# Second attention of a vision tower: where VectorE gives slots to routed tokens, and where TensorE turns the third group's outputs back

## The chip, the cores and the metric

The kernel runs on one core of a Trainium2 chip. Its time is the device time of one execution in microseconds (us), and a smaller time is better. Five engines work side by side and wait for one another through semaphores: TensorE (PE in the profile, with its weight loads as PEld), VectorE (DVE), ScalarE (ACT), GpSimd (POOL) and the queue of SyncE (SP), which issues DMAs.

## The reference, cut to what matters

32 sequences of 256 tokens with 256 features pass a token mixer, a first attention with 16 heads, and then a block with a latent attention and a mixture of eight experts. A class token is put ahead of each sequence, so a sequence has 257 rows. The change lies in the latent attention (called the second attention here), whose stage also does the routing for the experts.

```python
def _mla(h, Wq, Wdkv, Wuk, Wuv, Wo):
    q = (h @ Wq).reshape(B, S, HEADS, hd)          # 16 heads of 16
    c = h @ Wdkv                                   # latent of 128
    k = (c @ Wuk).reshape(B, S, HEADS, hd)
    v = (c @ Wuv).reshape(B, S, HEADS, hd)
    scores = jnp.einsum('bqhd,bkhd->bhqk', q, k) / jnp.sqrt(...)
    scores = jnp.where(causal, scores, -1000000000.0)
    a = jax.nn.softmax(scores, axis=-1)
    out = jnp.einsum('bhqk,bkhd->bqhd', a, v).reshape(B, S, D)
    return out @ Wo

def _moe(h, gate_w, w1, w2):
    logits = t @ gate_w
    top_v, top_i = jax.lax.top_k(logits, TOP_K)    # 2 of 8 experts
    gates = jax.nn.softmax(top_v, axis=-1)
    ...                                            # silu(t w1) w2, combined by the gates
x = x + _mla(_rmsnorm(x, g1), Wq, Wdkv, Wuk, Wuv, Wo)
x = x + _moe(_rmsnorm(x, g2), gate_w, w1, w2)
```

## The kernel before, in words

The program has stages that follow one another: constants and the token mixer with the first attention (to about 1700 us of the trace), a short stage for the class tokens, the second attention (`latent_attention`, about 1780 to 2890 us), the loading of the experts' weights, the experts, and the final output.

`latent_attention` goes through 32 samples (sequences). Samples 0 to 2 and 29 to 31 are written out; samples 3 to 28 run in a loop with two samples in its body. Each engine has its own `sample` function, and the order of the calls in it is the order of that engine's instructions; nothing else sets it. What keeps the engines in step are waits on semaphores.

The 16 heads of a sample are four groups (0 to 3) of four heads. A group goes through this chain:

- TensorE `scores` (L2118 mask, L2124 products) puts the scores of a group into PSUM banks 0 to 3. It first waits until ScalarE has read the previous group out of these banks (`exp_done`), the first two banks and the last two separately.
- VectorE `maxima` (L1852, two reductions) takes the row maxima out of the banks.
- TensorE `turn_maxima` (L2133) transposes them; VectorE `lower_queries` (L1857) adds them to the queries.
- TensorE `mask_keys` (L2139) and `lowered_scores` (L2148, L2153) compute the transposed scores less their maxima.
- ScalarE `powers` (L1722, L1723) takes the exponentials in two halves. `scores` of the next group can fill the banks from then on.
- TensorE `weigh` (L2168, L2171) applies them to the values, ScalarE `copy_output` (L1712) copies the result, TensorE `turn_back` (L2190) transposes it back, VectorE `divide` (L1863, L1865) divides by the row sums.

Between the links of this chain stand parts of other samples: TensorE computes the next sample's latents, keys, values and queries (`turn` L2022, `latent` L2029, `keys` L2040, `values`, `queries`), and for the sample before its output projection (`turn_output` L2197, `output` L2205) and its routing (`turn_tokens` L2079, `logits`, `counts`). `turn_back` and `divide` of groups 2 and 3 of a sample are done during group 0 of the next one.

The routing of the sample before the current one is a side line: VectorE `norm_tokens` (L1887) writes the normalised tokens, GpSimd `token_copy` (L1624, L1626) doubles them, VectorE `give_slots` (L1936 to L1947) turns ranks and counts into row numbers and gate weights, and GpSimd `scatter` (L1640) writes the rows to memory with four indirect DMAs, each issued when the one before has landed. GpSimd then goes on in its queue: `roots` (L66) and `keep` (L1613, L1614), which copy a sample's normalised rows away. VectorE's `normalise` (L1819, L1824) of the sample two ahead waits for both. VectorE's `choose` (L1899 to L1924), which ranks the experts, stands in group 2; `result` (L1875, L1876) stands ahead of it.

Of the kernel before, what the change touches and what calls it, by code (L numbers as in the profile page):

```python
# [1458 lines left out]
def latent_attention(nc, v, a, nb):  # L1459
# [5 lines left out]
    with ExitStack() as ctx:  # L1465
# [74 lines left out]
        def need(eng, sem, n):  # L1540

            if not isinstance(n, int) or n > 0:
                eng.wait_ge(sem, n)
# [12 lines left out]
        def sent(n):  # L1556

            return 64 * n + 32
# [237 lines left out]
        def _(dve):  # L1796
# [48 lines left out]
            def maxima(i, g, first=None):  # L1845

                dve.wait_ge(s_done, 4 * i + g + 1)
                for t in range(LT):
                    if t and first:
                        first(i)  # L1850
                    cols = slice(0, SEQ) if t else slice(SEQ, SEQ + 1 + P)
                    dve.tensor_reduce(nm[:, t, :, DK], ps[:, 0:4, cols], AX.X, ALU.max,  # L1852
                                      negate=True).then_inc(max_done, 1)

            def lower_queries(i, d, g):
                dve.wait_ge(nm_done, 4 * i + g + 1)
                dve.tensor_tensor(qx[:, g % 2], ps[:, OB + g % 2, L:2 * L], qT[:, d, g], ALU.add).then_inc(qx_done, 1)  # L1857

            def divide(i, g):
                bank = (BB, BA, BB, BB)[g]  # L1860
                dve.wait_ge(back_done, 4 * i + g + 1)
                out = ps[:, bank, 0:L].rearrange("p (t h r) -> p t h r", t=LT, h=4)
                dve.reciprocal(rec[:, g % 2], out[:, :, :, DK]).then_inc(rec_done, 1)  # L1863
                dve.wait_ge(rec_done, 4 * i + g + 1)
                dve.tensor_tensor(on[:, :, 4 * DK * g:4 * DK * (g + 1)].rearrange("p t (h d) -> p t h d", h=4),  # L1865
                                  out[:, :, :, 0:DK], rec[:, g % 2].unsqueeze(3).to_broadcast([P, LT, 4, DK]),
                                  ALU.mult).then_inc(on_done, 1)
# [14 lines left out]
            def norm_tokens(i, e, rows):  # L1882
                dve.wait_ge(r_rooted, i)
                if not isinstance(i, int) or i >= 3:
                    dve.wait_ge(rows_out, sent(i - 3))
                for t in range(LT):
                    dve.scalar_tensor_tensor(tn[:, e, 0, t, 0:MODEL], rows[:, t], ms[:, 2, t:t + 1], v.g2[:], ALU.mult,  # L1887
                                             ALU.mult).then_inc(z_done, 1)
# [37 lines left out]
            def place(i, d):  # L1926
                dve.wait_ge(counted, i - 1)
                need(dve, placed, i - 2)
                cnt = ps[:, CNB, FREE:FREE + (LT + 1) * NEXP].rearrange("p (t e) -> p t e", e=NEXP)
                dve.tensor_tensor(pos[:], cnt[:, 0:LT], v.fill[:, d].unsqueeze(1).to_broadcast([P, LT, NEXP]),  # L1930
                                  ALU.add).then_inc(slot_step, 1)
                dve.tensor_tensor(v.fill[:, 1 - d], cnt[:, LT], v.fill[:, d], ALU.add).then_inc(placed, 1)
# [16 lines left out]
            def sample(i, d, before, behind):  # L1949
                j, e = i + 1, 1 - d  # L1950
                maxima(i, 0, (lambda i: place(i, d)) if before >= 2 else None)
                lower_queries(i, d, 0)
                if before:
                    divide(i - 1, 2)
                    divide(i - 1, 3)
                if behind:
                    class_keys(j, e)
                if before:
                    norm_tokens(i, e, v.xcls if before == 1 else x)
                if before >= 2:  # L1960
                    give_slots(i, d)
                maxima(i, 1)
                lower_queries(i, d, 1)
                if behind:
                    last_value(j, e)
                if behind == 2:
                    norm_stats(i + 2, d)
                if before:
                    result(i - 1, e)
                maxima(i, 2, read_logits if before else None)  # L1970
                lower_queries(i, d, 2)
                if before:
                    choose(i)
                divide(i, 0)
                maxima(i, 3)
                lower_queries(i, d, 3)
                divide(i, 1)
                if behind:
                    last_key(j, e)
                if behind == 2:  # L1980
                    normalise(i + 2, d)
                if before:
                    mean_square(i)
# [32 lines left out]
        def _(pe):  # L2016
            def turn(j):
                pe.wait_ge(hn_done, LT * j + LT)
                need(pe, on_done, 4 * j - 6)
                for k in range(KT):  # L2020
                    for t in range(LT):
                        last = pe.transpose(ps[:, BA, k * L + t * P:k * L + (t + 1) * P], hn[:, t, k * P:(k + 1) * P],  # L2022
                                            v.ident[:])
                last.then_inc(hn_T, 1)
# [103 lines left out]
            def turn_maxima(i, g):  # L2128
                n = 4 * i + g
                pe.wait_ge(max_done, LT * n + LT)  # L2130
                need(pe, o_copied, n - 1)
                for t in range(LT):
                    last = pe.transpose(ps[:, OB + g % 2, L + t * P:L + (t + 1) * P],  # L2133
                                        nm[:, t].rearrange("p h r -> p (h r)"), v.ident[:])
                last.then_inc(nm_done, 1)
# [38 lines left out]
            def turn_back(i, g, more):  # L2174
                pe.wait_ge(o_copied, 4 * i + g + 1)
                bank = (BB, BA, BB, BB)[g]
                if g == 0:
                    need(pe, base_done, i)
                elif g == 1 and more:
                    pe.wait_ge(q_copied, 2 * i + 3)  # L2180
                elif g == 1:
                    pe.wait_ge(zT_done, i)
                elif g == 2 and more:
                    pe.wait_ge(q_copied, 2 * i + 4)
                elif g == 2:
                    pe.wait_ge(on_done, 4 * i + 1)
                elif g == 3:
                    pe.wait_ge(on_done, 4 * i + 3)
                for t in range(LT):
                    last = pe.transpose(ps[:, bank, t * P:(t + 1) * P], oa[:, g % 2, t * P:(t + 1) * P], v.ident[:])  # L2190
                last.then_inc(back_done, 1)
# [17 lines left out]
            def sample(i, d, before, behind):  # L2209
                j = i + 1  # L2210
                scores(i, d, 0, counts if before >= 2 else None)
                if before:
                    weigh(i - 1, 1 - d, 3)
                if behind:
                    turn(j)
                turn_maxima(i, 0)
                mask_keys(i, 0)
                lowered_scores(i, d, 0)
                if before:
                    turn_back(i - 1, 2, True)  # L2220
                if behind:
                    latent(j)
                if before:
                    turn_back(i - 1, 3, True)
                scores(i, d, 1)
                weigh(i, d, 0)
                if before:
                    turn_tokens(i, 1 - d, behind)
                    turn_output(i - 1)
                turn_maxima(i, 1)  # L2230
                mask_keys(i, 1)
                lowered_scores(i, d, 1)
                if behind:
                    last_values(j)
                    keys(j, 0)
                if before:
                    output(i - 1)
                scores(i, d, 2, logits if before else None)
                weigh(i, d, 1, behind > 0)
                if behind:  # L2240
                    values(j)
                turn_maxima(i, 2)
                mask_keys(i, 2)
                lowered_scores(i, d, 2)
                turn_back(i, 0, behind > 0)
                if behind:
                    queries(j, 0)
                scores(i, d, 3)
                weigh(i, d, 2)
                if behind:  # L2250
                    keys(j, 1)
                turn_maxima(i, 3)
                mask_keys(i, 3)
                lowered_scores(i, d, 3)
                turn_back(i, 1, behind > 0)
                if behind:
                    queries(j, 1)
# [534 lines left out]
```

## Time and profile before

| what | us |
|---|---|
| median of 3 runs (3506.6 to 3513.24) | 3507.42 |
| the profiled execution | 3506.24 |
| its span, first to last instruction | 3504.5 |
| TensorE busy in the span | 3098.7 (88%) |
| VectorE busy | 2078.0 (59%) |
| ScalarE busy | 1415.8 (40%) |
| GpSimd busy | 1186.6 (34%) |

The profile is of one execution. A row of the timeline tells when an instruction (or a merged run of equal ones) started, how long it was busy, and in brackets how long its engine had stood idle before it and which engine ended that wait. A time difference between rows of two engines can be read directly, since all share one clock. In the text a loop sample is followed in the stretch from 2327 to 2360 us, which is one sample (group 0's scores start at 2327.45 and the next sample's at 2360.01).

### The profile page before, as it was taken

Reading aid. Unit: us, or ns where it says so; the run is one execution under the profiler, and the core shown is the slowest. Engines: PE = TensorE matmul, PEld = TensorE weight load, DVE = VectorE, ACT = ScalarE, POOL = GpSimd, SP = SyncE. Lnnn points to the kernel's source line nnn. Section 1 sums busy time; section 2 is a strip of 40 time slices with the busy share of each in tenths; the row PEclk is TensorE's granted clock in tenths of the full one; section 3 lists DMA queues with packets and bytes.
Section 4 is the critical chain, followed back from the end, with each engine's and each line's share of the span. In section 5 each row is a group of like instructions: output and inputs, shape, how many; then the busy total and the mean of one; then the engine's idle time right before and its main releaser. Section 6 shows DMA issues by size and latency. Waiting matters only on the chain. (4 is left out here: it accounts for less than half of the span.)

```text
span 3504.5 us, 68873 instructions
## 1 busy us (share of the span) xinstructions
PE 3098.7 (88%) x22960; PEld 2325.7 (66%) x22961; DVE 2078.0 (59%) x5119; ACT 1415.8 (40%) x2884; POOL 1186.6 (34%) x1031
## 2 busy tenths in 40 slices
PE   3899999999999999999769999999999953999990
PEld 1667667666766666676437676677677733999990
DVE  4566666666665667567336666666666644444442
ACT  0444444444444444444314444444444423444440
POOL 2343443344344334434321222222222221444440
PEclk7999999999999999999879999999999976999995
DMA  3332232233233233323101111111111115444449
GB/s 76 79 91 66 68 90 78 60 87 88 65 71 90 73 65 87 88 62 74 45 20 31 37 44 42 35 44 45 33 42 45 37 38 162 78 76 78 76 77 299
DMA packets 219177, 249.00 MB, mean 71 GB/s; under 512 B 36129, under 2 KB 180834, under 8 KB 219122
## 3 DMA queue, kind: packets, MB, share of 16 engines
q1 hardware_dynamic: 184658, 204.82, 22.3%
q0 software_dynamic: 25936, 34.95, 6.0%
q10 hardware_dynamic: 8528, 8.52, 0.7%
q8 instruction: 32, 0.52, 0.1%
q14 instruction: 23, 0.19, 0.0%
HBM read 142.30 MB, written 105.87 MB: 71 GB/s over the span
## 5 line engine op out<-in xcount | busy, mean ns | idle before, releaser
L652 ACT ACTIVATE R<-psA 128x1024 f32<-128x1024 f32 x256 | 262.8, 1027 | 199.0 <-PE psA L1122 197.1
L838 DVE TENSOR_TENSOR PR<-R 128x1024 f32<-128x1024 f32 x256 | 312.8, 1222 | 0.0
L66 POOL TENSOR_TENSOR vrn<-vsm,inv_root 128x16 f32<-128x16 f32 x64 | 207.1, 3235 | 290.9 <-DVE vsm L823 289.7
L1137 PE MATMUL psA<-PR,V 128*64 128x258 f32 x2048 | 281.9, 396 | 0.0
L1852 DVE TENSOR_REDUCE m_nm<-psC 128x4 f32<-128x516 f32 (+1 forms) x256 | 239.2, 956 | 70.6 <-PE psC L2124 70.0
L1723 ACT ACTIVATE m_PT<-psC 128x770 f32<-128x770 f32 x256 | 197.6, 798 | 186.7 <-PE psC L2153 186.7
L657 ACT ACTIVATE oTs<-psA 128x258 f32<-128x258 f32 x256 | 98.8, 386 | 390.9 <-PE psA L1137 386.7
L1182 PE MATMUL psA<-wout,OT 128*128 128x256 f32 x1024 | 253.8, 391 | 0.4 <-DVE OT L880 0.4
L1640 POOL DMA_INDIRECT xg<-r_tn,r_idx x130 | 127.7, 983 | 281.4 <-DMA xg<-r_tn,r_idx 240.3
L1182 PEld LDWEIGHTS psA<-wout,OT 128*128 128x128 f32 x1024 | 185.5, 191 | 34.1 <-DVE OT L880 0.7
L66 POOL TENSOR_TENSOR orr<-osm,inv_root 128x32 f32<-128x32 f32 x32 | 174.3, 5447 | 42.4 <-DVE osm L852 42.4
L66 POOL TENSOR_TENSOR rstd<-rstd,inv_root 128x2 f32<-128x2 f32 x64 | 45.6, 712 | 413.6 <-DVE rstd L736 413.6
L1137 PEld LDWEIGHTS psA<-PR,V 128*64 128x64 f32 x2048 | 125.1, 137 | 85.6 <-issue 31.3
L1712 ACT ACTIVATE m_oa<-psC 128x256 f32<-128x256 f32 x128 | 49.1, 383 | 322.2 <-PE psC L2171 322.2
L1122 PE MATMUL psA<-qs,ks 64*128 64x256 f32 x1024 | 133.1, 339 | 47.1 <-DMA qs<-parts 47.1
L2446 POOL DMA_INDIRECT out_rows<-e_y,e_dest x69 | 106.8, 1548 | 188.6 <-DVE e_y L2507 185.3
L1122 PEld LDWEIGHTS psA<-qs,ks 64*128 64x128 f32 x1024 | 79.4, 191 | 133.8 <-issue 120.8
L836 DVE COPY PR<-acl 128x4 f32<-128x4 f32 x256 | 45.0, 176 | 177.0 <-ACT R L652 175.4
L2475 ACT ACTIVATE e_sh<-psE 128x512 fp32r<-128x512 f32 x137 | 81.9, 598 | 166.3 <-PE psE L2549 166.3
L2446 POOL DMA_INDIRECT xs<-e_y,e_dest x68 | 105.4, 1550 | 126.4 <-DVE e_y L2507 120.6
L2499 DVE TENSOR_TENSOR e_sl<-psE,e_sh 128x512 fp32r<-128x512 f32 x137 | 94.8, 692 | 75.2 <-ACT e_sh L2475 75.2
L2556 PE MATMUL psE<-w2h,e_sh 128*128 x548 | 132.7, 278 | 0.6 <-ACT e_sh L2475 0.6
(414 smaller groups left out, 8006.9 us busy)
## 6 DMA issues: line engine op xcount, KB each, us to landing
ks<-parts SPq DMA_DIRECT2D x512, 64.0 KB, 2.3
qs<-parts SPq DMA_DIRECT2D x512, 64.0 KB, 2.3
e_x<-xg SPq DMA_DIRECT2D x143, 129.0 KB
xraw<-in_x SPq DMA_DIRECT2D x66, 256.0 KB
xs<-m_zrow SPq DMA_DIRECT2D x32, 264.0 KB
f_even<-out_rows SPq DMA_DIRECT2D x13, 640.0 KB
f_odd<-xs SPq DMA_DIRECT2D x13, 640.0 KB
out_rows<-f_even ACTq DMA_DIRECT2D x13, 640.0 KB, 5.7
```

The source lines that it names most:

```text
L66: return pool.tensor_tensor(out, x, e.to_broadcast(list(out.shape)), ALU.pow)
L652: act.activation(R[:, p % 2], ps[:, 0:2, :].rearrange("p a (t n) -> p a t n", t=LT), ACT.Relu).then_inc(relu_done, 1)
L657: act.activation(oTs[:, d, p], ps[:, 2 + p % 2, 0:QCOLS], ACT.Copy).then_inc(o_copied, 1)
L838: dve.tensor_tensor(PR[:, p % 2, :, :, 0:L], R[:, p % 2], R[:, p % 2], ALU.mult).then_inc(prob_done, 1)
L1122: last = pe.matmul(ps[:, hh, t * L:(t + 1) * L], ks[rows, p, t * P:(t + 1) * P], qs[rows, p, :], start=True, stop=True, skip_group_check=True)
L1137: last = pe.matmul(ps[64 * hh:64 * hh + 64, 2 + p % 2, 0:QCOLS], V[:, d, t, n * DV:(n + 1) * DV], PR[:, p % 2, hh, t, :], start=False, sto ...
L1182: last = pe.matmul(ps[:, BOUT, t * MODEL:(t + 1) * MODEL], OT[:, m % 2, p % 2, t * P:(t + 1) * P], v.wout[:, p, :], start=p == 0 and t == ...
L1640: pool.indirect_dma_start(v.xg, bass.IndirectOffsetOnAxis(ap=idx[rows, d, s, t:t + 1], axis=0), tn[rows, d, s, t], None).then_inc(rows_out ...
L1723: act.activation(PT[:, g % 2, 2 * b:2 * b + 2, :], ps[:, 2 * b:2 * b + 2, 0:3 * P + 1], ACT.Exp).then_inc(exp_done, 1)
L1852: dve.tensor_reduce(nm[:, t, :, DK], ps[:, 0:4, cols], AX.X, ALU.max, negate=True).then_inc(max_done, 1)
L2446: pool.indirect_dma_start(v.odd if b % 2 else out, bass.IndirectOffsetOnAxis(ap=dest[:, b % XD:b % XD + 1], axis=0), y[:, b % XD], None, c ...
L2556: pe.matmul(ps[:, YB + d, 0:MODEL], sh[:, d, m], part(v.w2h, e, c, MODEL), start=m == 0, stop=False)
```

## The change

Two calls are moved; no instruction is added or taken away.

- VectorE's `give_slots(i, d)` stood between `norm_tokens` and `maxima(i, 1)`; it now stands behind `lower_queries(i, d, 1)`. This concerns the 30 samples 2 to 31.
- TensorE's `turn_back(i - 1, 2, True)` stood behind `lowered_scores(i, d, 0)`; it now stands ahead of `turn_maxima(i, 0)`. This concerns the 31 samples 1 to 31.

```diff
@@ VectorE, sample()
                 if before:
                     norm_tokens(i, e, v.xcls if before == 1 else x)
+                maxima(i, 1)
+                lower_queries(i, d, 1)
                 if before >= 2:
                     give_slots(i, d)
-                maxima(i, 1)
-                lower_queries(i, d, 1)
                 if behind:
                     last_value(j, e)
@@ TensorE, sample()
                 if behind:
                     turn(j)
+                if before:
+                    turn_back(i - 1, 2, True)
                 turn_maxima(i, 0)
                 mask_keys(i, 0)
                 lowered_scores(i, d, 0)
-                if before:
-                    turn_back(i - 1, 2, True)
                 if behind:
                     latent(j)
```

VectorE in the loop's first sample, before. L1887 is `norm_tokens`, L1936 to L1947 are `give_slots`, L1852 the maxima of group 1; ISA and REGISTER_ALU rows are waits and their counts.

```order
L1887 SCALAR_TENSOR_TENSOR r_tn<-m_x,r_ms,g2b 128x256 x2
L1935 ISA
L1936 TENSOR_TENSOR r_posab<-r_sab,r_pos 128x32
L1939 TENSOR_SCALAR r_es<-r_ex 128x2
L1940 REGISTER_ALU
L1941 TENSOR_REDUCE r_slot<-r_posab 128x4
L1943 RECIPROCAL r_tn<-r_es 128x2
L1944 REGISTER_ALU
L1945 CAST r_idx<-r_slot 128x4
L1947 TENSOR_TENSOR r_tn<-r_ex,r_tn 128x2
L1847 REGISTER_ALU
L1852 TENSOR_REDUCE m_nm<-psC 128x4 x2
```

The same place with the change:

```order
L1887 SCALAR_TENSOR_TENSOR r_tn<-m_x,r_ms,g2b 128x256 x2
L1847 REGISTER_ALU
L1852 TENSOR_REDUCE m_nm<-psC 128x4 x2
L1857 TENSOR_TENSOR m_qx<-psC,m_qT 128x256
L1935 ISA
L1936 TENSOR_TENSOR r_posab<-r_sab,r_pos 128x32
L1939 TENSOR_SCALAR r_es<-r_ex 128x2
L1940 REGISTER_ALU
L1941 TENSOR_REDUCE r_slot<-r_posab 128x4
L1943 RECIPROCAL r_tn<-r_es 128x2
L1944 REGISTER_ALU
L1945 CAST r_idx<-r_slot 128x4
```

The six instructions of `give_slots` have moved behind the maxima (L1852) and the lowered queries (L1857) of group 1; the next thing behind them is `last_value` (L1840).

TensorE in the loop's first sample, before. L2022 turns the next sample's rows (`turn`), L2133 is `turn_maxima` of group 0, L2139 to L2153 are `mask_keys` and `lowered_scores`, L2190 is `turn_back`.

```order
L2022 MATMUL psC<-ident,m_hn 128x128 x4
L2130 ISA
L1543 REGISTER_ALU
L2133 MATMUL psC<-ident,m_nm 128x128 x2
L2139 MATMUL psC<-causal_k,ident_bf 128x2x129 x4
L2145 REGISTER_ALU
L2148 MATMUL psC<-m_qx,m_kb 4x1
L2153 MATMUL psC<-m_qx,m_kT 128x256 x4
L2153 MATMUL psC<-m_qx,m_kT 128x129 x4
L2184 ISA
L2190 MATMUL psC<-ident,m_oa 128x128 x2
```

The same place with the change:

```order
L2022 MATMUL psC<-ident,m_hn 128x128 x4
L2184 ISA
L2190 MATMUL psC<-ident,m_oa 128x128 x2
L2130 ISA
L1543 REGISTER_ALU
L2133 MATMUL psC<-ident,m_nm 128x128 x2
L2139 MATMUL psC<-causal_k,ident_bf 128x2x129 x4
L2145 REGISTER_ALU
L2148 MATMUL psC<-m_qx,m_kb 4x1
L2153 MATMUL psC<-m_qx,m_kT 128x256 x4
L2153 MATMUL psC<-m_qx,m_kT 128x129 x4
```

The two transposes of `turn_back` for group 2 have moved ahead of the wait for group 0's maxima. The queues of ScalarE, GpSimd and SyncE have the same instructions in the same order as before.

## Rows read from the trace of the kernel before

**Rows 1.** Busy time by stretch: length, each engine (instructions), PE clock, DMA, GB/s.
```profile
500.00:900.00 400.00, 385.95 (x2273) 275.87 (x2273) 262.35 (x562) 180.62 (x357) 164.22 (x111) 0.98 0.32 75
...
1904.00:2750.30 846.30, 801.28 (x8378) 595.27 (x8377) 572.96 (x1639) 356.56 (x780) 219.64 (x286) 1.00 0.13 41
```
**Rows 2.** Timeline of TensorE, loop sample: start, busy, instruction, [idle before, releaser].
```profile
2331.10 0.44 PE L2133 MATMUL psC<-ident,m_nm 128*128 128x128 f32 x2 [0.50 <-DVE m_nm L1852]
...
2333.04 0.44 PE L2190 MATMUL psC<-ident,m_oa 128*128 128x128 f32 x2
2333.32 1.03 PE L2029 MATMUL psC<-m_hT,wdkv 128*128 128x256 f32 x4
...
2335.07 0.94 PE L2124 MATMUL psC<-m_kT,m_qT 32*128 32x257 f32 x16
...
2339.07 0.44 PE L2133 MATMUL psC<-ident,m_nm 128*128 128x128 f32 x2 [0.94 <-DVE m_nm L1852]
```
**Rows 3.** Timeline of VectorE, the same stretch, and the row of `normalise` (L1819).
```profile
2326.37 0.74 DVE L1819 TENSOR_SCALAR m_y<-m_h,m_mv,m_scale 128x256 f32<-128x256 f32 x2
...
2328.98 0.70 DVE L1852 TENSOR_REDUCE m_nm<-psC 128x4 f32<-128x516 f32 x1 [0.88 <-PE psC L2124]
...
2335.34 0.88 DVE L1887 SCALAR_TENSOR_TENSOR r_tn<-m_x,r_ms,g2b 128x256 f32<-128x256 f32 x2
2336.14 0.18 DVE L1936 TENSOR_TENSOR r_posab<-r_sab,r_pos 128x32 f32<-128x32 f32 x1
...
2337.19 1.82 DVE L1852 TENSOR_REDUCE m_nm<-psC 128x4 f32<-128x516 f32 x2
...
2341.73 0.41 DVE L1840 TENSOR_TENSOR m_vc<-psC,m_own 4x256 f32<-4x256 f32 x1 [1.76 <-PE psC L2055]
```
**Rows 4.** Timeline of TensorE in written-out sample 1, which has no `give_slots`.
```profile
1848.22 0.94 PE L2124 MATMUL psC<-m_kT,m_qT 32*128 32x257 f32 x16
...
1851.13 0.43 PE L2133 MATMUL psC<-ident,m_nm 128*128 128x128 f32 x2
```
**Rows 5.** Timeline of VectorE in sample 1: the maxima of group 1.
```profile
1849.23 1.83 DVE L1852 TENSOR_REDUCE m_nm<-psC 128x4 f32<-128x516 f32 x2
```
**Rows 6.** Timeline of TensorE's weight loads, loop sample: second half of the next mask.
```profile
2334.74 0.11 PEld L2118 LDWEIGHTS psC<-causal_q,ident_bf 128*128 128x128 bf16 x2 [0.20 <-ACT m_PT L1723]
```
**Rows 7.** Timeline of ScalarE, loop sample: second half of group 0's exponentials.
```profile
2333.91 0.78 ACT L1723 ACTIVATE m_PT<-psC 128x770 f32<-128x770 f32 x1
```
**Rows 8.** Timeline of TensorE in written-out samples 29 and 31: group 1's turned maxima.
```profile
2761.73 0.44 PE L2133 MATMUL psC<-ident,m_nm 128*128 128x128 f32 x2 [0.81 <-DVE m_nm L1852]
...
2826.22 0.44 PE L2133 MATMUL psC<-ident,m_nm 128*128 128x128 f32 x2 [0.67 <-DVE m_nm L1852]
```
**Rows 9.** Timeline of GpSimd, loop sample: first indirect DMA, and `keep`.
```profile
2338.26 1.06 POOL L1640 DMA_INDIRECT xg<-r_tn,r_idx  x1 [1.00 <-DVE r_tn L1947]
...
2350.74 1.26 POOL L1613 TENSOR_TENSOR m_hyk<-m_h,m_y 128x512 f32<-128x512 f32 x1
2351.95 0.60 POOL L1614 COPY m_yk<-m_y 128x512 f32<-128x512 f32 x1
```
**Rows 10.** Timeline of VectorE, loop sample: one instruction of `choose`.
```profile
2350.04 2.00 DVE L1906 TENSOR_TENSOR r_exs<-r_lg,r_mx 128x16 f32<-128x16 f32 x1
```
**Rows 11.** Timeline of GpSimd in written-out sample 29: fourth indirect DMA, and `keep`.
```profile
2773.71 0.96 POOL L1640 DMA_INDIRECT xg<-r_tn,r_idx  x1 [4.60 <-DMA xg<-r_tn,r_idx]
...
2775.72 1.26 POOL L1613 TENSOR_TENSOR m_hyk<-m_h,m_y 128x512 f32<-128x512 f32 x1
2776.94 0.60 POOL L1614 COPY m_yk<-m_y 128x512 f32<-128x512 f32 x1
```
**Rows 12.** Timeline of VectorE in sample 29: the maxima of group 3.
```profile
2776.69 1.83 DVE L1852 TENSOR_REDUCE m_nm<-psC 128x4 f32<-128x516 f32 x2 [2.05 <-PE psC L2124]
```
**Rows 13.** Timeline of GpSimd, end of the stage: last indirect DMA of sample 31.
```profile
2840.83 0.96 POOL L1640 DMA_INDIRECT xg<-r_tn,r_idx  x1 [2.37 <-DMA xg<-r_tn,r_idx]
```
**Rows 14.** Timeline of VectorE, end of the stage: `norm_tokens` behind sample 31.
```profile
2845.27 0.87 DVE L1887 SCALAR_TENSOR_TENSOR r_tn<-m_x,r_ms,g2b 128x256 f32<-128x256 f32 x2
```

## The prediction

> **What bounds the kernel now.** I read the busy time by stretch first, because the change touches one stage only. In the loop part of the second attention TensorE is busy 801.28 of 846.30 us at a granted clock of 1.00 [rows 1]; VectorE is busy 572.96 us of it. So TensorE sets the pace there, and 45 us (5%) is what its waits can give back in the loop. The stretch holds 26 samples, 846.30 / 26 = 32.55 us each. Next I read TensorE's timeline through one loop sample for brackets. Two stand there: 0.50 us before group 0's `turn_maxima` and 0.94 us before group 1's, both ended by VectorE's maxima (L1852) [rows 2]. Groups 2 and 3 have no bracket there. 0.50 + 0.94 = 1.44 us of the 45 / 26 = 1.73 us a sample. These two are what the change aims at, one edit each.
>
> Then I read the chain around each wait on the other engines, to see what ends last once the named cause is gone.
>
> **Part 1, `give_slots` behind the lowered queries.** It starts at 2336.14 and the maxima of group 1 start at 2337.19 [rows 3]: 1.05 us stand ahead of the maxima. Could the maxima start at 2336.14? They need the scores, which start at 2335.07 [rows 2]. Sample 1 has no `give_slots` and shows the bare chain: scores start 1848.22, maxima start 1849.23 (1.01 later), `turn_maxima` at 1851.13 [rows 4, 5], 2.91 us from scores to `turn_maxima`. In the loop the same distance is 2339.07 - 2335.07 = 4.00 us. TensorE does the same work between the two in both samples, and in sample 1 without a bracket. So the distance can fall by 4.00 - 2.91 = **1.09 us**. That is more than the bracket of 0.94, because the end of a matmul is modelled and they overlap; the difference of starts is the safer measure, and 0.94 is the lower end (0.94 x 26 = 24.4 us in the loop instead of 28.3).
>
> For 1.09 the VectorE queue must be free at 2335.07 + 1.01 = 2336.08. `norm_tokens` lets the next instruction start at 2336.14 [rows 3], 0.06 late. Part 2 cures this (below). With part 1 alone I get 1.09 - 0.06 = 1.03.
>
> From `turn_maxima` on everything in the sample hangs on this chain (turned maxima, lowered queries, lowered scores, exponentials, next scores), so the whole rest of the sample moves 1.09 us ahead. What must not be late:
>
> - `give_slots` itself. VectorE now does it behind `lower_queries`, where it has 1.76 us idle before `last_value` (L1840) [rows 3]. 1.05 to 1.13 us fit; 0.6 us is left. Cost on VectorE's chain: nothing. If that cover were gone, at most 1.1 us would come back.
> - The indirect DMAs. Nothing on TensorE waits for the slots in this sample, but GpSimd's queue does: `scatter`, then `roots` and `keep`. Today the first DMA starts 2338.26 - 2336.14 = 2.12 us after `give_slots` starts [rows 3, 9]. The idle stretch before L1840 begins at 2341.73 - 1.76 = 2339.97, which becomes 2338.88. So the first DMA starts at 2341.00, 2.74 us later, and `keep` ends at 2351.95 + 0.60 + 2.74 = 2355.29 [rows 9]. Who waits: `normalise` of the sample two ahead, at 2326.37 + 32.56 - 1.09 = 2357.84 [rows 3]. 2.5 us are left. The next load of rows and the next token root are due later still. Cost: nothing.
>
> **Where `keep` now falls.** Today it runs from 2350.74 to 2352.55 beside `choose`, and there one instruction on 16 elements (L1906) takes 2.00 us [rows 9, 10]: it ends just as L1613 ends. VectorE is held up by GpSimd's read of SBUF, about 2 us a sample, hidden today because the maxima of group 3 come later. After the change `keep` runs from 2353.48 to 2355.29. `choose` is over by then, and the maxima of group 3 run, from about 2353 to 2355. If they were held up, the wait would move to group 3 on the main chain. Sample 29 shows just that overlap: its third DMA took 4.60 us instead of about 2.4, `keep` ran from 2775.72 to 2777.54, and the maxima of group 3 ran from 2776.69 for 1.83 us [rows 11, 12], the same 1.83 as in sample 1 [rows 5]. So these reductions, which read PSUM, are not held up. Cost: nothing, and VectorE gains slack in group 2.
>
> The Trainium skill (SBUF, State Buffer; Who interferes with whom) says that a VectorE instruction with two SBUF inputs and a GpSimd instruction that reads SBUF exclude each other for its whole length, and that `tensor_reduce` on this chip never does. The trace agrees with both halves: 2.00 us for L1906, 1.83 for L1852. Read without the second half, the rule would speak against this change and give the first rival below.
>
> **Part 2, `turn_back` ahead of the maxima.** It takes 2333.32 - 2333.04 = 0.28 us of TensorE [rows 2]. In its new place it starts when `turn` (L2022) is through. The bracket of group 0's `turn_maxima` says 2331.10 - 0.50 = 2330.60; 2330.60 + 0.28 = 2330.88 is before 2331.10, so it fits into the wait of 0.50 us and `turn_maxima` is not late. What it needs (group 2's copied outputs, the bank freed by the copied queries) has been done since before the sample's first scores. Behind `lowered_scores` 0.28 us less stands before `scores` of group 1. But those do not start earlier: the second half of their mask waits for ScalarE's second exponential, which ends at 2333.91 + 0.78 = 2334.69, and the weight load comes at 2334.74 with a bracket of 0.20 [rows 6, 7]. The exponentials hang on the maxima of group 0 and not on `turn_back`. So TensorE trades one wait for another: bounds 0 and 0.28 us a sample, and I take **0**, since the bracket shows the wait to be there already. The one thing that it gives: `divide` of group 3, the class keys and `norm_tokens` on VectorE come 0.28 earlier, so that the 0.06 us above goes away.
>
> **The sum.** Loop, 26 samples x 1.09 = 28.3 us. Samples 2, 29 and 30, written out, have a shorter wait (0.81 in samples 29 and 30 [rows 8], about the same in sample 2), 0.13 less than 0.94: 3 x 0.96 = 2.9. Sample 31 has 0.67 [rows 8], 0.27 less, so 0.82; but behind it `norm_tokens` (2845.27) [rows 14] waits until all of sample 31's DMAs have landed. Their last one starts at 2840.83 [rows 13] and becomes some 2.6 us later, 2843.4, and lands some 2.4 us after that, at 2845.8: 0.6 us past today's 2845.27. So sample 31 gives between -0.6 and 0.8; I take 0. Together 28.3 + 2.9 + 0 = **31.2 us**. Behind the stage a barrier moves everything ahead by the same amount.
>
> The profiled execution took 3506.24 us, so 3475.0; the median of the runs is 1.2 us above it, so **3476 us**, 0.9% less.
>
> **The rivals.**
>
> *GpSimd's tensor work holds up group 3's maxima or lowered queries (slower).* Place: `keep` at 2353.48 to 2355.29 against the second reduction, which is due at about 2353.6. Price: it would start at 2355.29 instead of 2353.6, 1.7 us late, all of it on the chain, against the 1.09 gained: 0.6 us x 26 = 16 us lost in the loop, 3523. It decides from 1.09 us of hold-up a sample. Against it: sample 29. For it: only that the lowered queries (one SBUF input) have no such row; they come at about 2355.3, just as `keep` ends. 3 in 100.
>
> *The scatter stretches (no change, or slower).* The order in which indirect and other DMAs meet is new. In sample 29 one of them took 2.2 us more. One such stretch in every sample fits into the 2.5 us left; two (4.4 us) make `normalise` 1.9 us late, of which 0.9 us vanishes in VectorE's idle time before the next maxima [rows 3]: 1.0 us a sample, 26 in all, 3502. It begins to cost from 3.4 us of stretch and eats the gain from 4.5. Against it: in the loop these DMAs already run beside the writing of the output rows, and from the first of them to `keep` only 12.5 us pass [rows 9]. 5 in 100.
>
> *Part 2 gives its 0.28 us as well.* 31 x 0.28 = 8.7 us more, 3467. It needs the exponentials not to bound group 1's scores, against the bracket. 4 in 100.
>
> *The clock.* TensorE will be busy about 98% in the loop instead of 95. In the first attention the granted clock is 0.98 at 96% busy, here 1.00 [rows 1]. A fall to 0.98 would cost 2% of about 820 us, 16 us, 3492. Nothing in the rows says that more work brings the clock down, and nothing excludes it; 3 in 100.
>
> The forecast (1.0 to 1.1 us a sample) has 85 in 100. Its own width: 0.94 instead of 1.09 would give 4 us less, sample 31 some 1 us either way, and the runs of before differ by up to 6.6 us. That is 3471 to 3483. To leave no more than 2 in 10 out I widen it to **3468 to 3490**.
>
> This kernel's measurement tells about 0.2%, 7 us, from no change. Faster by more: 0.94. Within: 0.03. Slower: 0.03.
>
> **What would show it.** Right: in a loop sample the bracket before group 1's `turn_maxima` is gone or under 0.1 us and the step from L2124 to L2133 is 2.91; group 0 keeps a wait of 0.2 to 0.25; the weight load for the second half of group 1's mask waits about 0.5 us for ScalarE; a sample takes 31.46 us; no instruction of `choose` takes 2 us any more, and L1852 of group 3 stays at 1.83. Wrong: a bracket before group 3's `turn_maxima` (first rival), a bracket before L1819 named after GpSimd (second), the step from group 0's to group 1's scores shorter by 0.28 us (third), or a granted clock below 1.00 in the stage (fourth).

## The result, and the profile after

Both parts together make the kernel faster. The median of five runs is 3486.47 us (3480.35 to 3489.52), that of five runs of the kernel before 3513.24 us (3506.6 to 3523.51). The ratio is 0.9917 with a 95% interval of 0.9893 to 0.9942. In a second set on another occasion (below, e4) it is 0.9909 (0.9892 to 0.9925). One of the 13 runs of before in that set took 3673.23 us at a lower granted clock and is left out of the ratios. The forecast was 3476 against 3507.42, a ratio of 0.991.

The whole gain lies in the second attention. I take as its length the time from TensorE's first turned maxima to GpSimd's first instruction in the next stage. The busy time by stretch between these two points, before (columns as in [rows 1]):

```profile
1815.79:2894.61 1078.82, 982.05 (x10258) 728.67 (x10258) 689.49 (x2007) 435.35 (x954) 269.39 (x355) 0.98 0.12 39
```

And after:

```profile
1821.48:2868.26 1046.78, 978.32 (x10258) 730.83 (x10258) 625.02 (x2007) 435.93 (x954) 267.31 (x355) 0.98 0.12 40
```

The stage is 1078.82 - 1046.78 = **32.0 us** shorter. TensorE has the same work (982 and 978 us), so the gain is idle time that is gone. VectorE is busy 64 us less, of which more below. The span fell by only 3504.5 - 3478.6 = 25.9 us, because the stage begins 5.7 us later (1821.48 against 1815.79). The stages ahead have the same instructions in both kernels, so I put this down to variation from run to run and not to the change: e4, the changed kernel once more, began the stage at 1818.7. With one trace of before it is likely and not shown.

TensorE's timeline of one loop sample, after. It answers to [rows 2]:

```profile
2318.30 0.94 PE L2124 MATMUL psC<-m_kT,m_qT 32*128 32x257 f32 x16
2320.27 0.66 PE L2022 MATMUL psC<-ident,m_hn 128*128 128x128 f32 x4
2320.77 0.38 PE L2190 MATMUL psC<-ident,m_oa 128*128 128x128 f32 x2
2321.42 0.43 PE L2133 MATMUL psC<-ident,m_nm 128*128 128x128 f32 x2 [0.28 <-DVE m_nm L1852]
...
2323.36 1.13 PE L2029 MATMUL psC<-m_hT,wdkv 128*128 128x256 f32 x4
2324.33 0.38 PE L2190 MATMUL psC<-ident,m_oa 128*128 128x128 f32 x2
...
2325.39 0.94 PE L2124 MATMUL psC<-m_kT,m_qT 32*128 32x257 f32 x16
...
2328.29 0.43 PE L2133 MATMUL psC<-ident,m_nm 128*128 128x128 f32 x2
...
2349.71 0.94 PE L2124 MATMUL psC<-m_kT,m_qT 32*128 32x257 f32 x16
```

The bracket of 0.94 before group 1's turned maxima is gone; from scores to turned maxima it is 2328.29 - 2325.39 = 2.90 us instead of 4.00. Group 0 keeps 0.28 of its 0.50. The sample takes 2349.71 - 2318.30 = 31.41 us instead of 32.56. Over the 26 loop samples the mean is 31.42 against 32.54.

VectorE's timeline of the same stretch, which answers to [rows 3]:

```profile
2316.69 0.74 DVE L1819 TENSOR_SCALAR m_y<-m_h,m_mv,m_scale 128x256 f32<-128x256 f32 x2
...
2325.45 0.88 DVE L1887 SCALAR_TENSOR_TENSOR r_tn<-m_x,r_ms,g2b 128x256 f32<-128x256 f32 x2
2326.39 1.83 DVE L1852 TENSOR_REDUCE m_nm<-psC 128x4 f32<-128x516 f32 x2
2328.76 0.43 DVE L1857 TENSOR_TENSOR m_qx<-psC,m_qT 128x256 f32<-128x256 f32 x1 [0.53 <-PE psC L2133]
2329.10 0.18 DVE L1936 TENSOR_TENSOR r_posab<-r_sab,r_pos 128x32 f32<-128x32 f32 x1
...
2330.95 0.41 DVE L1840 TENSOR_TENSOR m_vc<-psC,m_own 4x256 f32<-4x256 f32 x1 [1.04 <-PE psC L2055]
```

The maxima start 1.00 us after the scores, `give_slots` follows at 2329.10, and 1.04 us idle are left ahead of `last_value`.

TensorE's weight loads at the second half of group 1's mask, which answers to [rows 6]:

```profile
2325.06 0.11 PEld L2118 LDWEIGHTS psC<-causal_q,ident_bf 128*128 128x128 bf16 x2 [0.41 <-ACT m_PT L1723]
```

GpSimd, which answers to [rows 9]:

```profile
2330.89 1.06 POOL L1640 DMA_INDIRECT xg<-r_tn,r_idx  x1 [3.53 <-DVE r_tn L1947]
...
2343.31 1.26 POOL L1613 TENSOR_TENSOR m_hyk<-m_h,m_y 128x512 f32<-128x512 f32 x1
2344.53 0.60 POOL L1614 COPY m_yk<-m_y 128x512 f32<-128x512 f32 x1
```

VectorE's maxima of group 3 beside it, which answers to [rows 12]:

```profile
2343.24 1.83 DVE L1852 TENSOR_REDUCE m_nm<-psC 128x4 f32<-128x516 f32 x2 [2.12 <-PE psC L2124]
```

`keep` now runs beside these maxima, and they still take 1.83 us, as in all 26 loop samples. `choose` is clear of it: VectorE's instructions of line L1906 in the whole program after (minimum, median, maximum in ns), where [rows 10] had one of 2.00 us:

```profile
L1906 DVE TENSOR_TENSOR r_exs<-r_lg,r_mx x33: 165/168/170, 1867.8 to 2841.7; 128x16 f32<-128x16 f32 x33
```

This line gives 10 us of VectorE's 64. With the other lines of `choose` (L1903 21 us, L1900 11, L1909 7 and smaller ones) it is 56 us, and 10 more are `give_slots`, above all its cast L1945 (sums of durations, which overlap a little). Together that is about 2 us a sample of being held up. [rows 10] show one case: L1906 began at 2350.04, while GpSimd's `roots` (L66) ran from 2349.56 to 2350.75, and ended with L1613, which followed at once. These times were never on the path, as VectorE's brackets now show idle time in their place (2.12 before group 3's maxima, where before there was none).

### The profile page after: what moved, and what is told of

It is laid out like the page before. It is cut to its first block and busy times, and to the rows that moved or that the text cites. A ratio compares the mean times of both kernels' runs of the same rounds, so it can differ in the third digit from the quotient of the medians.

```text
span 3478.6 us, 68873 instructions
## 1 busy us (share of the span) xinstructions
PE 3098.7 (89%) x22960; PEld 2329.3 (67%) x22961; DVE 1996.9 (57%) x5119; ACT 1417.1 (41%) x2884; POOL 1190.2 (34%) x1031
## 5 line engine op out<-in xcount | busy, mean ns | idle before, releaser
L66 POOL TENSOR_TENSOR vrn<-vsm,inv_root 128x16 f32<-128x16 f32 x64 | 218.1, 3408 | 289.9 <-DVE vsm L823 289.8
L1852 DVE TENSOR_REDUCE m_nm<-psC 128x4 f32<-128x516 f32 (+1 forms) x256 | 239.5, 958 | 129.3 <-PE psC L2124 127.9
L66 POOL TENSOR_TENSOR orr<-osm,inv_root 128x32 f32<-128x32 f32 x32 | 174.4, 5449 | 43.0 <-DVE osm L852 43.0
L66 POOL TENSOR_TENSOR rstd<-rstd,inv_root 128x2 f32<-128x2 f32 x64 | 45.7, 714 | 414.8 <-DVE rstd L736 414.8
```

What stands on the lines that cost most here:

```text
L66: return pool.tensor_tensor(out, x, e.to_broadcast(list(out.shape)), ALU.pow)
```

## The experiments

The theory behind the prediction: group 1's maxima were late by what stood ahead of them on VectorE, part 1 removes that, and part 2 gives TensorE nothing of its own because ScalarE's exponentials set the next scores. The rival for part 2: its 0.28 us are TensorE's own. Lengths of a loop sample below are means of samples 3 to 28, and the stage is measured as above.

| kernel | loop sample | stage | ratio to before (95%) |
|---|---|---|---|
| before | 32.54 | 1078.8 | |
| both parts | 31.42 | 1046.8 | 0.9917 (0.9893 to 0.9942) |
| e1 slots alone | 31.48 | 1048.0 | 0.9908 (0.9891 to 0.9925) |
| e2 turn_back alone | 32.32 | 1072.0 | 0.9983 (0.9974 to 0.9993) |
| e3 place split | 31.35 | 1044.7 | 0.9911 (0.9894 to 0.9927) |
| e4 both again | 31.41 | 1046.4 | 0.9909 (0.9892 to 0.9925) |
| e5 slots behind norm_stats | 32.09 | 1069.4 | one run, 3499.57 us |
| e6 slots behind result | 34.07 | 1123.2 | one run, 3562.7 us |
| e7 short exponential | 31.27 | 1040.9 | one run, 3483.15 us |

The one run of before beside e5 to e7 took 3514.42 us; these three are read from their traces.

The start of the stage lay anywhere from 1815.8 to 1830.0 us in these nine traces. The same kernel gave 31.42 and 31.41 us a sample and 1046.8 and 1046.4 us of stage in two traces (both parts, e4). Differences of 0.05 us a sample can therefore be read from the sample and the stage, and not from the total.

### e1: part 1 alone

```diff
@@ TensorE, sample(), against the changed kernel
                 if behind:
                     turn(j)
-                if before:
-                    turn_back(i - 1, 2, True)
                 turn_maxima(i, 0)
                 mask_keys(i, 0)
                 lowered_scores(i, d, 0)
+                if before:
+                    turn_back(i - 1, 2, True)
```

> give_slots behind the lowered queries, turn_back left where it was. Theory (the maxima of group 1 are the path; part 2 only frees the last 0.06 us of VectorE's queue): a loop sample goes from 32.56 to 31.5 us, 0.05 to 0.07 more than with both parts (31.41); the step from group 1's scores to its turned maxima is 2.96 to 2.98 instead of 2.90; the stage gives back 29.5 to 30.5 us of the 32.0 that both parts give. Rival (part 2 brings TensorE time of its own, 0.28 us a sample): a loop sample takes 31.69 us and the stage gives back about 23.5 us.

Measured: 31.48 us a sample and 1078.8 - 1048.0 = 30.9 us in the stage, against 32.0 for both. Part 1 is nearly all of it; the stage gave 0.4 us more than the upper end of what was expected. The rival with 31.69 falls. TensorE's timeline of e1:

```profile
2319.27 0.94 PE L2124 MATMUL psC<-m_kT,m_qT 32*128 32x257 f32 x16
2322.39 0.43 PE L2133 MATMUL psC<-ident,m_nm 128*128 128x128 f32 x2 [0.49 <-DVE m_nm L1852]
...
2326.35 0.94 PE L2124 MATMUL psC<-m_kT,m_qT 32*128 32x257 f32 x16
2329.31 0.44 PE L2133 MATMUL psC<-ident,m_nm 128*128 128x128 f32 x2
```

From group 0's scores to group 1's it is 2326.35 - 2319.27 = 7.08 us, with both parts 2325.39 - 2318.30 = 7.09. The 0.28 us that part 2 takes from between them is not there. From scores to turned maxima it is 2.96 against 2.90: the 0.06 that `norm_tokens` is late without part 2.

### e2: part 2 alone

```diff
@@ VectorE, sample(), against the changed kernel
-                maxima(i, 1)
-                lower_queries(i, d, 1)
                 if before >= 2:
                     give_slots(i, d)
+                maxima(i, 1)
+                lower_queries(i, d, 1)
```

> turn_back of group 2 ahead of the maxima, give_slots left where it was. Theory (VectorE's divisions, norm_tokens and give_slots stand in a row ahead of group 1's maxima, and all of them come 0.28 us earlier): group 0's to group 1's scores stays 7.09 us, group 1's scores to turned maxima falls from 4.00 to 3.72, a loop sample takes 32.28 us, the stage gives back about 8 us. Rival a (it is TensorE's own 0.28 us): the first of the two steps is the one that gets shorter, to 6.81. Rival b (the edit is worth nothing alone): 32.56 us a sample.

Measured: 32.32 us a sample, 6.8 us in the stage where about 8 was expected, a ratio of 0.9983 (0.9974 to 0.9993). Rival b falls. TensorE's timeline of e2 tells the other two apart:

```profile
2332.73 0.94 PE L2124 MATMUL psC<-m_kT,m_qT 32*128 32x257 f32 x16
...
2335.19 0.38 PE L2190 MATMUL psC<-ident,m_oa 128*128 128x128 f32 x2
2335.85 0.44 PE L2133 MATMUL psC<-ident,m_nm 128*128 128x128 f32 x2 [0.28 <-DVE m_nm L1852]
2338.76 0.38 PE L2190 MATMUL psC<-ident,m_oa 128*128 128x128 f32 x2
2339.82 0.94 PE L2124 MATMUL psC<-m_kT,m_qT 32*128 32x257 f32 x16
...
2343.61 0.44 PE L2133 MATMUL psC<-ident,m_nm 128*128 128x128 f32 x2 [0.72 <-DVE m_nm L1852]
```

Group 0's to group 1's scores: 2339.82 - 2332.73 = 7.09, unchanged. Group 1's scores to its turned maxima: 3.79 instead of 4.00. So the gain comes over VectorE: `divide` of group 3 and all behind it are earlier, up to the maxima. The two parts act on the same 1.1 us, and their effects don't add: alone they give 1.06 and 0.22 us a sample, together 1.12.

The size was expected as 0.28 and is 0.21. `latent` (L2029) takes 2324.33 - 2323.36 = 0.97 us to the next start in the changed kernel, where it follows the lowered scores directly, and 0.97 in e2 too; it took 0.88 behind `turn_back` (2334.20 - 2333.32, of which [rows 2] has the first). So 0.09 of the 0.28 us go to it; why the next start comes later there I have not tested.

### e3: one instruction less between group 0's maxima

Group 0 still waits 0.28 us for its maxima. `place` reads the expert counts from PSUM bank 1 between the two reductions, because TensorE writes that bank again as soon as the maxima are done. Here one copy stays there. TensorE's next write of that bank then waits for the copy (`counts_read`) and no longer for `placed`; the excerpt leaves that line and the new buffer out.

```diff
+            def read_counts(i):
+                dve.wait_ge(counted, i - 1)
+                need(dve, placed, i - 2)
+                cnt = ps[:, CNB, FREE:FREE + (LT + 1) * NEXP].rearrange("p (t e) -> p t e", e=NEXP)
+                dve.tensor_copy(cns[:], cnt).then_inc(counts_read, 1)
...
-                maxima(i, 0, (lambda i: place(i, d)) if before >= 2 else None)
+                maxima(i, 0, read_counts if before >= 2 else None)
                 lower_queries(i, d, 0)
+                if before >= 2:
+                    place(i, d, False)
```

> The changed kernel, and between the two reductions of group 0 VectorE only copies the counts out of PSUM (one instruction instead of two); the two additions of place stand behind the lowered queries, where VectorE is idle for 2.0 us. Theory (group 0's maxima are still waited for, by 0.28 us): one start-to-start step of 0.08 us less on the path, a loop sample 31.33 instead of 31.41, 2.4 us in the stage. Rival (TensorE's own queue or ScalarE's copy of outputs sets group 0's turned maxima, and the maxima are not the last): no change, 31.41.

Measured: 31.35 us a sample (most of them 31.34), 0.07 less than with both parts, and a stage 1.7 to 2.1 us shorter than in e4 and the first trace. TensorE's timeline of e3 (L2135 is L2124, L2144 is L2133):

```profile
2319.93 0.94 PE L2135 MATMUL psC<-m_kT,m_qT 32*128 32x257 f32 x16
...
2322.99 0.43 PE L2144 MATMUL psC<-ident,m_nm 128*128 128x128 f32 x2 [0.21 <-DVE m_nm L1854]
```

From group 0's scores to its turned maxima it is 3.06 us instead of 2321.42 - 2318.30 = 3.12, and the bracket fell from 0.28 to 0.21. The theory holds: group 0's maxima are on the path. In the total it can't be told from the changed kernel: 3482.36 us (3481.15 to 3483.44) against 3481.05 (3476.99 to 3484.73) in the same set.

### e4: both parts again

> Both parts, as the changed kernel has them, for a second trace beside the others. Expected: a loop sample of 31.41 us again, and the stage's start anywhere within some 6 us of before, since the stages ahead of it have the same instructions in both kernels.

Measured: 31.41 us a sample, the stage 1046.4 us, its start at 1818.7. The median of its four runs is 3481.05 us, that of 13 runs of before in the same set 3513.49.

### e5 and e6: how much slack GpSimd's queue has

The prediction gave the delayed DMAs 2.5 us until `normalise` and another 0.9 until the next maxima. In the trace after, `keep` ends at 2344.53 + 0.60 = 2345.13, and `normalise` follows 31.39 us behind its row of 2316.69, at 2348.08: 2.95 us. In the 26 loop samples it is between 2.6 and 3.5 us, in e4 between 2.1 and 3.6, since the landing of the DMAs varies. These two kernels use it up.

```diff
@@ e5: VectorE, sample(), give_slots taken from its place in the changed kernel
                 if behind == 2:
                     norm_stats(i + 2, d)
+                if before >= 2:
+                    give_slots(i, d)
                 if before:
                     result(i - 1, e)
```

> The changed kernel with give_slots still later on VectorE, behind the statistics of the sample two ahead (norm_stats). The slots come about 3.9 us later than in the changed kernel, and so do the DMAs and keep. Theory (GpSimd's queue has 3.1 us left before normalise is due, and VectorE another 0.9 before the next maxima): no cost or up to 0.1 us a sample, 31.4 to 31.5 us; normalise is about 0.8 us late and gets a bracket that names GpSimd. Rival (no slack is left, or the scatter stretches): over 31.9 us a sample.

```diff
@@ e6: the same, one call further
                 if before:
                     result(i - 1, e)
+                if before >= 2:
+                    give_slots(i, d)
```

> The changed kernel with give_slots behind result, another 2.1 us later (about 6.0 us later than in the changed kernel). Theory (3.1 + 0.9 us of slack, then each us costs a us in each sample): 2.0 us a sample more, 33.4 us, the stage 50 us longer and slower than before the change; a bracket before normalise names GpSimd's keep or roots. Rival (the next thing takes up the delay, as when only every second sample is hit): under 32.4 us a sample.

e5 measured 32.09 us a sample: 0.67 more, where 0 to 0.1 was expected. GpSimd's timeline of e5:

```profile
2312.07 1.05 POOL L1640 DMA_INDIRECT xg<-r_tn,r_idx  x1 [7.46 <-DVE r_tn L1947]
2316.20 0.96 POOL L1640 DMA_INDIRECT xg<-r_tn,r_idx  x1 [3.07 <-DMA xg<-r_tn,r_idx]
2319.44 0.96 POOL L1640 DMA_INDIRECT xg<-r_tn,r_idx  x1 [2.28 <-DMA xg<-r_tn,r_idx]
...
2324.85 1.26 POOL L1613 TENSOR_TENSOR m_hyk<-m_h,m_y 128x512 f32<-128x512 f32 x1
2326.06 0.60 POOL L1614 COPY m_yk<-m_y 128x512 f32<-128x512 f32 x1
```

SyncE's queue of e5 in the same stretch:

```profile
2312.69 0.38 SPq L1572 DMA_DIRECT2D out_rows<-m_base  x1
2313.26 0.32 SPq L1586 DMA_DIRECT2D xs<-m_zrow  x1
```

The direct part was sized rightly: in sample 3, the first of the loop and not yet late itself, the first DMA starts 3.95 us later in the sample. But SyncE now issues the writing of the output rows (256 KB, and 264 KB of `xs` behind it) 0.5 to 0.6 us after it, and the wait behind it grows to 3.07 us (3.41 and 3.23 in the next two samples, 3.0 to 3.5 in all) from 2.3 to 2.75. From the first DMA to `keep` it is mostly 12.6 to 13.4 us instead of 12.0 to 12.8. So 3.9 + 0.4 to 0.9 meets a slack of 3.0 + 0.9, and the rest is on the path. That the two writes cause the longer wait is argued from their place; no edit moved them alone. But e6 bears it out: there they are issued 1.5 and 0.9 us ahead of the first DMA, the wait behind it is 2.4 to 2.7 us, and from it to `keep` it is 12.0 to 12.6 us. VectorE's timeline of e5 shows the wait:

```profile
2324.79 0.21 DVE L1863 RECIPROCAL m_rec<-psC 128x8 f32<-128x8 f32 x1 [1.52 <-PE psC L2190]
2325.03 0.29 DVE L1865 TENSOR_TENSOR m_on<-psC,m_rec 128x128 f32<-128x128 f32 x1
2325.24 0.91 DVE L1834 TENSOR_TENSOR m_kb<-m_kT,blk 128x16 f32<-128x16 f32 x1
2326.70 0.74 DVE L1819 TENSOR_SCALAR m_y<-m_h,m_mv,m_scale 128x256 f32<-128x256 f32 x2 [0.55 <-POOL m_yk L1614]
```

It also shows side by side which instructions GpSimd holds up. While GpSimd's L1613 ran (2324.85 to 2326.11), L1865 with one input in PSUM and one in SBUF took its usual 0.29 us, and L1834 with both inputs in SBUF took 0.91 until that instant.

e6 measured 34.07 us a sample: 2.65 more, where 2.0 was expected, and the stage is 1123.2 us, longer than before the change. Of the 26 loop samples the first, ahead of any delay, takes 31.48 us. Of the other 25, 14 take 33.05 to 33.47, as expected with 2.0 us more, and 11 take 34.3 to 36.0. TensorE's timeline of one of the latter:

```profile
2324.62 0.65 PE L2022 MATMUL psC<-ident,m_hn 128*128 128x128 f32 x4 [0.95 <-DVE m_hn L1824]
2325.11 0.38 PE L2190 MATMUL psC<-ident,m_oa 128*128 128x128 f32 x2
2326.58 0.68 PE L2133 MATMUL psC<-ident,m_nm 128*128 128x128 f32 x2 [1.09 <-DVE m_nm L1852]
...
2328.18 1.67 PE L2153 MATMUL psC<-m_qx,m_kT 32*128 32x256 f32 x16
```

The busy time of that stretch, cut at the point where the matmuls get slow and where they are fast again (PE clock is the third number from the end):

```profile
2326.40:2333.00 6.60, 6.42 (x34) 4.40 (x34) 1.53 (x8) 1.93 (x4) 0.00 (x0) 0.50 0.00 0
2333.00:2355.00 22.00, 21.79 (x233) 16.41 (x233) 13.96 (x45) 8.77 (x20) 4.20 (x7) 1.00 0.13 42
```

With these two waits of 0.95 and 1.09 us the granted clock went to 0.50, the lower level (1.2 GHz), and the sixteen matmuls of L2153 took 1.67 us instead of the 0.94 that they take at the upper one. The 11 longer samples all have such a stretch of the lower clock, the other 14 have none; against the 33.26 us that these 14 take on average, it costs 1.0 to 1.4 us in four samples and 2.4 to 2.7 in seven. What it comes from is only in part shown. No loop sample without late `normalise` has it, in this trace or that of the change. But all 25 late samples have both waits, the second of them always 1.09 us, and the same waits as above left the clock at 1.00 in sample 24. Its two rows of TensorE, and the busy time of a stretch of three and a half samples around it:

```profile
2667.06 0.65 PE L2022 MATMUL psC<-ident,m_hn 128*128 128x128 f32 x4 [0.95 <-DVE m_hn L1824]
...
2669.01 0.43 PE L2133 MATMUL psC<-ident,m_nm 128*128 128x128 f32 x2 [1.09 <-DVE m_nm L1852]
...
2620.00:2735.00 115.00, 106.08 (x1118) 79.36 (x1116) 66.70 (x217) 47.83 (x105) 31.52 (x40) 1.00 0.13 40
```

So the lateness of `normalise` has a second price that I had not counted, in some samples and not in others, and the length of the two waits does not decide in which. e5 paid it once, in written-out sample 30 (35.89 us).

### e7: a shorter exponential

```diff
                 for b in range(2):
...
-                    act.activation(PT[:, g % 2, 2 * b:2 * b + 2, :], ps[:, 2 * b:2 * b + 2, 0:3 * P + 1],
+                    n = L if b and g == 0 and not (isinstance(i, int) and i == 0) else 3 * P + 1
+                    act.activation(PT[:, g % 2, 2 * b:2 * b + 2, 0:n], ps[:, 2 * b:2 * b + 2, 0:n],
                                    ACT.Exp).then_inc(exp_done, 1)
```

> The changed kernel, leaving out of group 0's second exponential the last third of the columns in samples 1 to 31 (256 of 385 in each bank). Theory (the second half of group 1's mask waits for this exponential): the exponential falls from 0.79 to about 0.53 us, group 0's to group 1's scores from 7.09 to about 6.83; behind it norm_tokens on VectorE becomes the last at group 1's maxima, 0.14 us after the point that was the scores', so a loop sample gives back about 0.14 us, 31.27. Rival (TensorE's queue sets the scores of group 1): 7.09 stays and the sample keeps 31.41.

This kernel leaves the last 129 of 385 columns in each of the two banks uncomputed, so its output is not that of the reference; it serves only to time the wait.

Measured: 31.27 us a sample, 0.15 less than 31.42. TensorE's timeline of e7 (its lines stand one higher: L2125 is L2124, L2134 is L2133):

```profile
2324.32 0.94 PE L2125 MATMUL psC<-m_kT,m_qT 32*128 32x257 f32 x16
...
2331.20 0.94 PE L2125 MATMUL psC<-m_kT,m_qT 32*128 32x257 f32 x16
2334.15 0.44 PE L2134 MATMUL psC<-ident,m_nm 128*128 128x128 f32 x2
```

Group 0's to group 1's scores fell to 2331.20 - 2324.32 = 6.88 us, by 0.21, when the exponential got 0.22 shorter (0.57 instead of 0.79 us). From there to the turned maxima it is 2.95 again, since `norm_tokens` is now the last. That the exponential bounds group 1's scores is thereby shown, and with it why part 2 gives TensorE nothing: a shorter exponential moves these scores, as do earlier maxima ahead of it (7.02 in e3), and 0.28 us less of TensorE's work does not (e1 against both parts).

## Why the prediction was right, point by point

**What bounds.** Right. TensorE's work in the stage stayed the same and the time fell by its waits. TensorE is now busy 98% of the loop at a granted clock of 1.00, so the clock rival did not come about:

```profile
1904.00:2722.00 818.00, 799.91 (x8378) 598.85 (x8378) 512.41 (x1639) 357.42 (x781) 217.58 (x286) 1.00 0.13 42
```

**Part 1, 1.09 us a sample.** Right. The step from scores to turned maxima fell from 4.00 to 2.90 us (forecast 2.91). Sample 1, which has no `give_slots`, was a good stand-in. With part 1 alone I had worked out 1.03; e1 gave 1.06.

**Covers.** `give_slots` fits into the idle time ahead of `last_value`: 1.04 us are left where 0.6 was forecast, since it got shorter too (from 1.05 to 0.8 us, without GpSimd's copies beside it). `keep` ends 2.95 us before `normalise` instead of 2.5. No cost from either, as said. The maxima of group 3 were not held up, so the first rival falls with 26 samples of evidence instead of one. Lowered queries, for which the prediction had no row, met `keep` in a few samples: in e4 they ran at 2342.41 inside `keep`'s copy (L1614, 2342.20 to 2342.80) and took 0.42 us as elsewhere. That half of the rival falls too.

**Part 2.** Right as worked out, in both halves: zero for TensorE, shown by e1, e2 and e7, and 0.06 us through VectorE's queue. The bounds were 0 and 0.28; with the bracket of 0.20 on one weight load I had taken the lower one. The bracket is now 0.41. The growth is less than 0.28 because `latent` takes 0.09 longer. About 0.5 us had been named for it. For group 0's wait 0.2 to 0.25 had been named, and it is 0.28: in its new place `turn_back` took 0.22 us of that wait and not 0.28.

**The sum.** 31.2 us forecast, 32.0 measured in the stage: 26 x 1.12 = 29.0 in the loop (28.3 forecast), 2.6 in samples 2, 29 and 30 (2.9), 0.4 in sample 31 and the end (0).

**The time.** 3476 was forecast and 3486.47 measured, inside 3468 to 3490 but 10 us off. The change itself is not what was mis-sized. Some 6 us of it are the base: I took the median of three runs, 3507.42, and it was low; five runs gave 3513.24 and thirteen 3513.49. The profiled execution of before had the earliest start of the second attention of all nine traces. With 3513.49 as the base, less 32.0, the result would be 3481.5, and e4 measured 3481.05. The other 5 us are the spread of the changed kernel's own runs (3486.47 in the first set, 3481.05 in e4), whose cause stays open.

**The scatter rival.** It did not come about here. But its threshold, 3.4 us of lateness before it costs, was tested by e5 and e6. It held as to the slack (3.0 + 0.9). Two things came on top that it lacked: a delay that puts the first DMA just ahead of the output rows brings a stretch of 0.4 to 0.9 us (e5), and a late `normalise` can bring the lower clock (e6).

## What to carry to other kernels

Where the busiest engine waits for a result, look at what stands in the queue of the engine that gives it, between its last need and that result. Work that no one on the path waits for goes behind, into the next idle stretch of that engine; a sample or iteration that lacks this work can tell the gain (here the step to 0.01 us, 2.91 against 2.90). Then measure the slack of whatever waits for the moved work: 3.9 us further behind it cost 0.67 us a sample (e5), and 6.0 us cost 2.65 (e6). Before adding up two such moves, ask whether they shorten the same wait: here 1.06 and 0.22 us made 1.12. And read a gain of 1% from the length of the stage in the trace, since here the median of before moved by 6 us, a fifth of the gain, from three runs to thirteen.

## What the runs showed of the hardware

- VectorE's two-input instructions with both inputs in SBUF stood still while GpSimd's tensor instruction ran (L1834 0.91 us instead of 0.17). Those with one input in PSUM did not (L1865 0.29), nor did reductions from PSUM (L1852 1.83). This is as the Trainium skill (SBUF, State Buffer; Who interferes with whom) has it. The cast of `give_slots` (L1945), with one input, took 0.45 us beside GpSimd's copy L1624 in the loop of before and 0.17 without it in the changed kernel. Moving the two apart made 64 us of VectorE's busy time vanish without any effect on the total.
- With TensorE waits of 0.75 to 1.28 us and 1.09 us, their ends 2 us apart, the granted clock fell to 0.50 in 11 of 25 loop samples of e6, during the second wait or within 0.2 us of it, and stayed at 1.00 in the other 14; 0.95 and 1.09 stand on both sides. In the loop of before, waits of 0.50 and 0.94, 8 us apart [rows 2], left the clock at 1.00 in all samples [rows 1].
- The wait behind the first indirect DMA was 3.0 to 3.5 us in the loop samples of e5, where writes of 256 and 264 KB from SyncE's queue were issued 0.5 to 1.2 us behind it, 2.3 to 2.75 in the changed kernel, where they come 4.4 us or more behind it, and 2.4 to 2.7 in e6, where they come 1.5 and 0.9 us ahead of it.
